# A preLN graph layer on one core: last batch's sums on another queue, its backward product by halves, two first batches reordered

## What is computed

```python
A_fwd = [adj, adj, shifted]                  # shifted = roll(eye, 1, axis=0)
A_list = A_fwd + [swapaxes(a, 1, 2) for a in A_fwd] + [eye]
HW = einsum('bnf,rfo->rbno', h, W[:, :F]) + einsum('rd,rdo->ro', W_edges, W[:, F:])[:, None, None, :]
out = x + max(einsum('rbnm,rbmo->rbno', A, HW), axis=0) + b
```

## Time and profile before

| | us |
|---|---|
| three runs | 214.88, 215.05, 215.61 |
| median | 215.05 |
| the profiled execution | 214.69 |
| its span, from first to last instruction | 212.9 |
| busy: PE, DVE, ACT, POOL | 203.8, 195.0, 182.8, 168.2 |
| TensorE's granted clock | 1.0 throughout |

### The profile page before, as it was taken

One profiled execution on the slowest core, in us unless ns is written; L12 is line 12 of the kernel. 1 busy time (PEld: TensorE's weight loads), 2 busy tenths in 40 slices (PEclk: granted clock), 3 DMA queues, 4 the chain that ended last, 5 costly groups with the idle time before them and its releaser, 6 DMA issues.

```text
span 212.9 us, 5004 instructions
## 1 busy us (share of the span) xinstructions
PE 203.8 (96%) x1003; PEld 165.4 (78%) x1003; DVE 195.0 (92%) x416; ACT 182.8 (86%) x453; POOL 168.2 (79%) x181
## 2 busy tenths in 40 slices
PE   7899998999999999999999999999999999999972
PEld 5677786877888888888888888888888888888851
DVE  4799779999999999999999999999999999989754
ACT  4779999699898989899998989999898989998360
POOL 1356869959797997979798897979799797979340
PEclk9999999999999999999999999999999999999999
DMA  6999879896998889797989989897988988053614
GB/s 226 299 334 198 123 153 293 187 278 97 338 158 250 190 241 248 180 269 124 292 161 236 211 213 272 170 261 132 261 184 215 251 191 229 3 143 57 145 53 99
DMA packets 117776, 42.38 MB, mean 199 GB/s; under 512 B 97287, under 2 KB 107527, under 8 KB 117767
## 3 DMA queue, kind: packets, MB, share of 16 engines
q1 hardware_dynamic: 113728, 33.11, 68.6%
q10 hardware_dynamic: 4039, 9.17, 13.6%
HBM read 38.00 MB, written 4.26 MB: 199 GB/s over the span
## 4 chain that ended last, share of the span: by engine, by line
PE 78%; DVE 6%; issue 4%; ACT 4%; DMA 4%; ACTq 1%; POOL 1%; DVEq 0%; POOLq 0%
PE rel_ps L880 11%; PE rel_ps L882 10%; PE rel_ps L881 10%; PE at_ps L857 9%; PE fwd_ps L880 6%; PE fwd_ps L882 6%; PE fwd_ps L881 6%; PE bwd_ps L882 6%; PE bwd_ps L880 6%; PE bwd_ps L881 5%; PE turn_ps L865 3%; DVE best L699 2%; DMA sum_all<-sums_dram 2%; DMA x_sb<-in_x 1%; ACT rel_ps L505 1%
## 5 line engine op out<-in xcount | busy, mean ns | idle before, releaser
L341 POOL TENSOR_TENSOR a_lo<-a_sb,a_hi 128x512 fp32r<-128x512 f32 x61 | 78.2, 1304 | 21.7 <-ACT a_hi L429 21.7
L505 ACT ACTIVATE rel_ps<-sum_all,c_col 128x512 f32<-128x512 f32 (+1 forms) x63 | 41.9, 685 | 10.5 <-DVE best L699 6.2
L699 DVE TENSOR_TENSOR best<-rel_ps,best 128x512 f32<-128x512 f32 x62 | 42.3, 682 | 2.3 <-PE rel_ps L882 1.7
L429 ACT ACTIVATE a_hi<-a_sb 128x512 fp32r<-128x512 f32 x64 | 39.5, 633 | 2.0 <-DMA a_sb<-in_adj 2.0
L670 DVE TENSOR_TENSOR at_lo<-at_ps,at_hi 128x512 fp32r<-128x512 f32 x48 | 32.7, 684 | 2.8 <-ACT at_hi L442 2.5
L442 ACT ACTIVATE at_hi<-at_ps 128x512 fp32r<-128x512 f32 x48 | 28.3, 591 | 5.7 <-PE at_ps L857 5.1
L880 PE MATMUL fwd_ps<-at_hi,h_hi 128*128 128x512 f32 x64 | 26.7, 417 | 0.7 <-issue 0.5
L880 PE MATMUL bwd_ps<-a_hi,h_hi 128*128 128x512 f32 x64 | 26.5, 414 | 0.0
L857 PEld LDWEIGHTS at_ps<-ident,a_sb 128*128 128x128 f32 x184 | 22.0, 141 | 4.6 <-issue 0.4
L857 PE MATMUL at_ps<-ident,a_sb 128*128 128x128 f32 x184 | 25.3, 272 | 0.0
L882 PE MATMUL fwd_ps<-at_hi,h_lo 128*128 128x512 f32 x64 | 25.3, 395 | 0.0
(11 more groups left out here) (107 smaller groups left out, 473.1 us busy)
## 6 DMA issues: line engine op xcount, KB each, us to landing
a_sb<-in_adj SPq DMA_DIRECT2D x28, 512.0 KB, 4.3
sum_all<-sums_dram ACTq DMA_DIRECT2D x16, 512.0 KB, 5.0
x_sb<-in_x SPq DMA_DIRECT2D x16, 256.0 KB, 5.2
xp_sb<-in_x SPq DMA_DIRECT2D x60, 64.0 KB, 3.2
out<-o_sb SPq DMA_DIRECT2D x60, 64.0 KB, 4.4
a_blocks<-in_adj SPq DMA_DIRECT2D x56, 64.0 KB, 2.1
a_sb<-in_adj SPq DMA_DIRECT2D x6, 256.0 KB, 4.5
sums_dram<-sum_rows ACTq DMA_DIRECT2D x56, 1.0 KB
```

What stands on the lines that cost most here:

```text
L341: pool.tensor_tensor(a_lo[q][:, j, :], a_sb[q][:, j, :], a_hi[q][:, j, :].bitcast(fp32), ALU.subtract).then_inc(a_lo_ready[j], 1)
L429: act.activation(a_hi[q][:, j, :], a_sb[q][:, j, :], ACT.Copy, accum_out=sums[q][:, j:j + 1]).then_inc(a_hi_ready[j], 1)
L505: act.activation(to[:, cols], sum_all[q][:, 0 if r in FWD else 1, cols], ACT.Copy, scale=c_col[:, r:r + 1]).then_inc(after_it, 1)
L699: dve.tensor_tensor(best[q][:], held[:], best[q][:], ALU.max).then_inc(joined[r], 1)
```

## The change

Five things are changed.

1. In the last step VectorE turns the sums ahead of the split of the last turned block (`turn_sums` between `split_at` 2 and 3), and SP, not ScalarE, stores and spreads the sums of batch 15. SP does this ahead of storing the output of batch 13; the load of the bias by nodes also comes ahead of that.
2. The `bwd` product of batch 15 is made in two halves of the nodes, half 0 in `bwd_ps` and half 1 in `turn_ps`, chunk by chunk between the relations of batch 14. Rounding, split and the relations 3 and 4 follow by halves, each in a bank of its own (`half_bank`).
3. The joins of batch 15 are ordered: relation 0, halves 0 of relations 3 and 4, relation 1 whole, halves 1 of relations 3 and 4. TensorE and ScalarE follow that order.
4. In batches 0 and 1: ScalarE rounds the first turned block ahead of the last chunk of a, spreads the sums of batch 0 behind the next block, and stores those of batch 1 behind all of normalise; VectorE does bn_stats of batch 3 ahead of taking the sums, and bn_aggr behind `split_ht`.
5. SP waits for the store of batch 0's sums ahead of `load_a_blocks(1, 0)`.

```diff
-        half_filled, half_done, half_stored = sem("half_filled"), sem("half_done"), sem("half_stored")
+        half_stored = sem("half_stored")
...
+        bwd_half_done, bwd_half_hi_ready, bwd_half_lo_ready = (
+            pair(sem, s) for s in ("bwd_half_done", "bwd_half_hi_ready", "bwd_half_lo_ready"))
+        half_done = {r: pair(sem, f"half_done{r}_") for r in BWD}
+        half_filled = {r: pair(sem, f"half_filled{r}_") for r in BWD}
+        part_joined = sem("part_joined")
+        bwd_half = (bwd_ps, turn_ps)
+
+        half_bank = {BWD[0]: (fwd_ps, rel_ps[BANK[FWD[0]]]), BWD[1]: (rel_ps[BANK[EYE[2]]], fwd_ps)}
...
+
+        def store_sums(queue, k, q):
+
+            queue.wait_ge(sum_rows_ready, 2 * k + q + 1)
+            for g in range(G):
+                queue.dma_start(sums_dram[q][:, g * Q:(g + 1) * Q],
+                                sum_rows[q][g * Q:g * Q + S, :]).then_inc(sums_stored[q], 16)
+
+        def spread_sums(queue, k, q):
+
+            queue.wait_ge(sums_stored[q], 16 + G * 16 * k)
+
+            wait(queue, filled[BWD[1]], 2 * k + q - 1)
+            queue.dma_start(sum_all[q][:].rearrange("p t n -> p (t n)"),
+                            sums_dram[q].rearrange("s p -> (s p)").unsqueeze(0).to_broadcast([P, 2 * N])
+                            ).then_inc(sums_spread[q], 16)
...
                 reload_x(0, 0)
                 reload_a(0, 0)
+
+                sp.wait_ge(sums_stored[0], 16)
                 load_a_blocks(1, 0)
...
             step(PAIRS - 1, 0, False)
-            step(PAIRS - 1, 1, False)
 
             sp.wait_ge(a_lo_ready[0], B - 1)
             sp.wait_ge(a_turned[C - 2], B - 1)
             sp.dma_start(last_bias.rearrange("p (c o) -> p c o", o=O), by_nodes(bias)).then_inc(bias_by_nodes_loaded, 16)
+
+            store_sums(sp, PAIRS - 1, 1)
+            spread_sums(sp, PAIRS - 1, 1)
+            step(PAIRS - 1, 1, False)
             store(PAIRS - 1, 0)
             store_half(sp, 0)
...
                 for j in range(C):
-                    if is_batch(b, 2) and j == C // 2:
-                        store_first_sums(1)
                     last = act.activation(h_sb[q][:, j, :], x_sb[q][:, j, :], ACT.Relu,
                                           bias=shift[q][:, j:j + 1], scale=rstd[q][:, j:j + 1])
                 last.then_inc(h_ready, 1)
...
-                spread_sums(0, 0)
                 round_at(*ahead, 2)
+                spread_sums(act, 0, 0)
                 round_ht(*ahead)
                 round_at(*ahead, 3)
                 round_a(*ahead, 0)
...
                     normalise(*ahead)
-                if not second:
-                    store_sums(k, q)
+                if second:
+                    store_first_sums(1)
+                elif left:
+                    store_sums(act, k, q)
                 act.wait_ge(joined[FWD[0]], b)
                 fill(*prev, BWD[0], rel_ps[BANK[BWD[0]]], filled[BWD[0]])
...
             round_a(0, 0, 2)
+            round_at(0, 0, 0)
             round_a(0, 0, 3)
-            for i in range(C):
+            for i in range(1, C):
                 round_at(0, 0, i)
             round_ht(0, 0)
...
+            def round_bwd_half(half):
+                act.wait_ge(bwd_half_done[half], 1)
+                act.activation(bwd_hi[:, half_cols(half)], bwd_half[half][:, half_cols(half)],
+                               ACT.Copy).then_inc(bwd_half_hi_ready[half], 1)
+
             act.wait_ge(joined[BWD[0]], B - 1)
             fill(k, q, FWD[0], rel_ps[BANK[FWD[0]]], filled[FWD[0]])
+            act.wait_ge(fwd_lo_ready, B)
+            fill(k, q, BWD[0], half_bank[BWD[0]][0], half_filled[BWD[0]][0], half_cols(0))
+            act.wait_ge(rel_done[BWD[1]], B - 1)
+            round_bwd_half(0)
             act.wait_ge(joined[BWD[1]], B - 1)
             fill(k, q, FWD[1], rel_ps[BANK[FWD[1]]], filled[FWD[1]])
-            act.wait_ge(fwd_lo_ready, B)
-            fill(k, q, BWD[0], fwd_ps, filled[BWD[0]])
-            round_bwd(k, q)
             act.wait_ge(joined[EYE[2]], B)
-            fill(k, q, BWD[1], rel_ps[BANK[EYE[2]]], half_filled, slice(0, HALF))
-            act.wait_ge(bwd_lo_ready, B)
-            fill(k, q, BWD[1], bwd_ps, filled[BWD[1]], slice(HALF, N))
+            fill(k, q, BWD[1], half_bank[BWD[1]][0], half_filled[BWD[1]][0], half_cols(0))
+            round_bwd_half(1)
+            act.wait_ge(joined[FWD[0]], B)
+            fill(k, q, BWD[0], half_bank[BWD[0]][1], half_filled[BWD[0]][1], half_cols(1))
+            act.wait_ge(part_joined, 1)
+            fill(k, q, BWD[1], half_bank[BWD[1]][1], half_filled[BWD[1]][1], half_cols(1))
             store_half(act, 1)
...
+            def split_bwd_half(half):
+
+                dve.wait_ge(bwd_half_hi_ready[half], 1)
+                dve.tensor_tensor(bwd_lo[:, half_cols(half)], bwd_half[half][:, half_cols(half)],
+                                  bwd_hi[:, half_cols(half)].bitcast(fp32), ALU.subtract).then_inc(bwd_half_lo_ready[half], 1)
...
                     split_at(k, q, 2)
+                    if not left:
+                        turn_sums(k, q)
                     split_at(k, q, 3)
-                    turn_sums(k, q)
+                    if left:
+                        turn_sums(k, q)
...
                 join(*prev, FWD[0])
                 if is_batch(b, 1):
+                    moments(k + 1, q)
                     take_sums()
                     join(*prev, FWD[1])
...
                     split_fwd(k, q)
-                if left > 1:
+                if left > 1 and not is_batch(b, 1):
                     moments(k + 1, q)
                 join(*prev, BWD[0])
                 if left > 1:
                     dve.wait_ge(bn_done, b + 3)
                 if left:
                     split_at(*ahead, 1)
-                if left > 1:
+                if left > 1 and not is_batch(b, 1):
                     mean_and_variance(q)
                 if left:
                     split_fwd(k, q)
+                if not left:
+                    split_bwd_half(0)
                 join(*prev, BWD[1])
                 if left:
                     split_ht(*ahead)
                 else:
                     turn_best(*prev)
+                if is_batch(b, 1):
+                    mean_and_variance(q)
                 join(k, q, EYE[2])
                 if left:
                     turn_best(*prev)
...
-            split_bwd(k, q)
+            split_bwd_half(1)
             join(k, q, FWD[0])
-            join(k, q, FWD[1])
-            join(k, q, BWD[0], fwd_ps)
-            dve.wait_ge(joined[BWD[0]], B)
-            for half, (held, done, count) in enumerate(((rel_ps[BANK[EYE[2]]], half_done, 1),
-                                                        (bwd_ps, rel_done[BWD[1]], B))):
...
+            dve.wait_ge(joined[FWD[0]], B)
+
+            def join_half(r, half, joined_ahead, joined_now):
+                cols = half_cols(half)
+                dve.wait_ge(half_done[r][half], 1)
+                dve.wait_ge(*joined_ahead)
+                dve.tensor_tensor(best[q][:, cols], half_bank[r][half][:, cols], best[q][:, cols],
+                                  ALU.max).then_inc(joined_now, 1)
+
+            join_half(BWD[0], 0, (joined[FWD[0]], B), part_joined)
+            join_half(BWD[1], 0, (part_joined, 1), part_joined)
+            dve.wait_ge(part_joined, 2)
+            dve.wait_ge(rel_done[FWD[1]], B)
+            dve.tensor_tensor(best[q][:], rel_ps[BANK[FWD[1]]][:], best[q][:], ALU.max).then_inc(half_joined[0], 1)
+            join_half(BWD[0], 1, (half_joined[0], 1), part_joined)
+            join_half(BWD[1], 1, (part_joined, 3), half_joined[1])
...
+            def bwd_half_chunk(half, j):
+
+                q = 1
+                if half == 0:
+                    if j == 0:
+                        pe.wait_ge(h_hi_ready, B)
+                        pe.wait_ge(h_lo_ready, B)
+                        pe.wait_ge(bwd_lo_ready, B - 1)
+                    pe.wait_ge(a_hi_ready[j], B)
+                    pe.wait_ge(a_lo_ready[j], B)
+                elif j == 0:
+                    pe.wait_ge(ht_lo_ready, B)
+                cols = half_cols(half)
+                last = passes(bwd_half[half][:, cols], h_hi[q][:, j, :], h_lo[q][:, j, :],
+                              a_hi[q][:, j, cols], a_lo[q][:, j, cols], j == 0, j == C - 1)
+                if j == C - 1:
+                    last.then_inc(bwd_half_done[half], 1)
...
+                elif not left:
+                    bwd_half_chunk(0, 0)
+                    bwd_half_chunk(0, 1)
+                    along(*prev, BWD[0])
+                    bwd_half_chunk(0, 2)
+                    bwd_half_chunk(0, 3)
+                    along(*prev, BWD[1])
+                    bwd_half_chunk(1, 0)
+                    bwd_half_chunk(1, 1)
+                    eye(k, q, EYE[2])
+                    bwd_half_chunk(1, 2)
+                    bwd_half_chunk(1, 3)
```

(24 more changed lines are left out.)

19 lines of the change are left out of this document (3 added, 16 removed).

## The result

| | before | after |
|---|---|---|
| median of six runs | 215.09 us (214.43 to 215.61) | 212.94 us (212.62 to 213.59) |
| ratio, with 95% interval | | 0.9904 (0.9878 to 0.9930) |
| profiled execution, and its span | 214.69, 212.9 | 212.62, 210.8 |
| busy: PE, DVE, ACT, POOL | 203.8, 195.0, 182.8, 168.2 | 203.9, 193.1, 183.8, 168.9 |

The direction was right and the size wrong: 212.94 lies 0.56 us under the range. The end cost what its sum said. The start gained 2.16 us where 1.0 was forecast.

What follows compares the result with a forecast made beforehand. TensorE, busy for 96% of the span, was taken as the bound, so gains must come from the first batches or the end: 214.69 - 1.0 + 0.25 = 213.94 us profiled, 214.3 against the median, range 213.5 to 215.6.

Steps and rivals of the forecast that it cites:

- The end, +0.25 forecast: Last batch: first fill 2.3 us sooner, but 8.65 us instead of 6.13 from it to the last join: 0.25 us net cost.
- the prediction's own list of signs of being wrong: Signs: TensorE waits for a_sb or h_lo, first fill waits for the spread, gaps in the middle, no idle VectorE before half split.
- The rival of a gain at the end: Last batch: half instructions overlap better, the end gives 0.3 and the start its full 1.15, total 213.6 us; chance 15%.
- the late landing: Last batch: sums land at 201.4 and the end costs 0.8, total 214.9 us; one case of the cancelling rival, 25%.
- The start, 1.0 forecast: First batches: 1.15 us gained by ScalarE's and VectorE's order, 0.15 taken off for the adjacency of batch 3.
- spread of batch 0 behind at_hi 2, and the gate: First batches: moving the spread frees ScalarE of 0.5, but its landing (18.2 and the median 5.0) stays the bound: no gain.
- ScalarE's and VectorE's order, "1.15 us": Batches 1 and 2: uninterrupted normalise and moved bn_stats and bn_aggr bring VectorE's results sooner; TensorE gains 1.15 us.
- adjacency of batch 3, "I take 0.15 off": SP's later loads bring the adjacency at 38.5 instead of 36.3, just when TensorE wants it; 0.15 us taken off.
- The product of 34.65: TensorE, batch 2: this product, which waited for VectorE, was to start at about 33.5, a gain of 1.15 us.
- The first rival (216.0): SP's gate frees nothing: loads come 3.8 us later, batch 3's adjacency at 40.1, start loses 0.5 to 0.9; chance 15%.
- The rule on the order of completions: Skill's rule: a semaphore's increment lands only after all earlier writes of that DMA engine across queues; then the gate frees 1.6 us.
- the turn at 32.33: TensorE's turn in batch 2, 0.60 us long, taken as floor: the work behind it starts at 32.8 instead of 33.41.

Runs made afterwards that it cites:

- bn_pool: Changed kernel with the statistics steps (bn_stats, bn_aggr) back in their old places on VectorE and GpSimd's wait in all batches: 213.38 us, ratio 0.9919.
- after_pool: Changed kernel plus GpSimd's wait for VectorE's difference of the turned quarter in all batches: 212.70 us, ratio 0.9885.
- pool_waits: Kernel before plus one wait: in batches 2 to 15 GpSimd starts its differences only after VectorE's of the turned quarter: 213.81 us, ratio 0.9916.
- cast_first: Kernel before, but in batch 1 GpSimd does its sum of input and bias behind the difference of the features: 215.02 us, ratio 0.9988.
- no_gate: Changed kernel without SP's wait for the store of the first sums: 213.62 us, ratio 0.9933.

## Why the prediction was right or wrong

**The end, +0.25 forecast, +0.27 measured (17.13 against 16.86).** Right in size at each step: rows ready sooner, issue by SP, landing near 3.8 (3.96), first fill 2.3 sooner (198.89 from a mark at 190.32 is 8.57, before 10.73: 2.16), 8.65 us of queue behind it (8.56), VectorE idle 1.5 and 0.8 (1.68 and 0.85). One thing is otherwise, and it is on the prediction's own list of signs of being wrong: the first fill does wait for the spread, 0.95 us. The forecast had batch 14's relation 3 as the later of the two; its join ended at 198.63, the spread landed at 198.81. That is where the 0.14 went that the fill lacks of its 2.3. The means of all profiles, 16.96 against 16.72, bear out the cost. The rival of a gain at the end fell with it, as did the late landing.

**The start, 1.0 forecast, 2.16 measured.** The failed step is this sum. It put the first mark at nothing, it had no term at all for the length of VectorE's instructions beside GpSimd's, and its other two terms were 0.14 and 0.15 short:

| step of the prediction | forecast | measured | what the runs showed |
|---|---|---|---|
| spread of batch 0 behind at_hi 2, and the gate: "its landing stays the bound there: nothing" | 0 | 0.39 | first fill at 22.71 instead of 23.08, spread issued at 17.41 instead of 18.23; ten profiles with the new order have a median turn of 32.0, seven with the old one 32.65 |
| ScalarE's and VectorE's order, "1.15 us" | 1.15 | 1.29 | "1 to 2"; bn_stats and bn_aggr are 0.65 of it (bn_pool against after_pool) |
| not in the sum: VectorE's SBUF instructions beside GpSimd | 0 | 0.48 | "2 to 3" and "3 to 4"; pool_waits gives 0.50 there |
| adjacency of batch 3, "I take 0.15 off" | -0.15 | 0 | issued 3.6 later (forecast 2.2), but under way for 5.3 us, not 7.3: there at 37.85, 0.1 ahead of the transposes |
| sum | 1.00 | 2.16 | |

The first term fails by the prediction's own numbers. It had the store of the first sums land at 16.6 instead of 18.2, and still let the spread, which waits for that store, start from 18.2. In the kernel before ScalarE stood 0.50 us for that store and 0.18 for the spread; in the changed kernel it stands for neither, but for 0.06 us ahead of the fill.

The second was right. The product of 34.65 was forecast 1.15 sooner, and came at 33.08, 1.18 sooner behind its turn. The rest of the 1.29 is the restart: after a wait TensorE's next product begins 0.33 behind (34.65 to 34.98), without one 0.23.

The third is the one that could have been read. The row of 1.74 us stood in the trace beside 48 of 0.65 to 0.69 with PSUM as input and twelve of its own kind of 0.68 to 0.70, and I took the 1.79 of the last batch as the instruction's own length. One shortcut of 1.07 us in VectorE's queue became 0.5 on TensorE.

The Trainium skill, "SBUF — State Buffer", section "Who interferes with whom", says that a VectorE instruction with two inputs in SBUF contends with one of GpSimd that reads SBUF, and that a cast can be in a mode that contends with GpSimd too, where whoever issues first has the shared ports for its whole instruction and the other blocks. By that rule the cast of 27.88 would wait for GpSimd's row of 27.59, to 28.89, and then take its 0.43: an estimate of 1.44 from its start. The trace has 1.30, so it agrees to 0.14 us. pool_waits and cast_first are what shows it here.

The fourth was near the edge. The adjacency was there 0.1 us ahead of its use in this execution, the fastest of six, and in five of the nine profiles with the gate it was late by 0.13 to 0.76. That nothing was lost here is luck; the limit that the prediction feared is real.

**The gate.** Forecast: the store of the first sums lands at 16.6 instead of 18.2. With the gate SP's next load shows the landing, since it waits for it: 15.92 in the changed kernel, 15.8 to 17.5 in the nine profiles with it. So the store was indeed sooner there. But the start doesn't gain all of that: ScalarE's queue reaches the spread at 17.4 only, and without the gate (no_gate) the store had landed by then as well. So it isn't shown that the gate is what made the store sooner. The first rival (216.0) named the right place, the adjacency of batch 3, but had it under way for as long as before; issued 3.6 later it landed 2.0 sooner after its issue. The rule on the order of completions that the prediction weighed is neither borne out nor refuted by these runs.

**Chances.** 43% for faster was too little for a start whose second term was right; the likeliest cases all put the start at 1.15 at most, because the turn at 32.33 was taken as a floor that the change can't move. It moved by 0.39.

**What remains open.** What the gate is worth, what SP's queue is worth without the early turn, why a later adjacency lands quicker, and how much of the first mark is the change: the spread was issued between 17.54 and 18.50 in the seven profiles with the old order, between 17.41 and 18.36 in the ten with the new one, so the 0.39 of one pair of profiles may be partly chance.

## What to carry to other kernels

Where one operation on one shape has two lengths in a trace, look at what GpSimd (or VectorE) had begun just before: the longer one is a lost race, and a wait on the engine that has time to spare can win it for the other. A gain in such a length counts only where somebody waits for it, so try it at the place where the chain passes. Before the difference of two stretches is given to an edit, look for a wait at their end that belongs to something else: here the adjacency, up to 0.76 us. A split made finer for overlap is worth nothing if its first piece stands in an ordered queue ahead of work that is ready; move the piece behind that work first, and then see whether the finer split still pays.

## What the hardware showed that I had not expected

- A 128x512 difference of VectorE from two SBUF tiles took 0.66 to 0.69 us alone and 1.60 to 1.80 where GpSimd's had begun first; the cast of the same size 0.43 against 1.27 to 1.54, and 0.68 to 0.82 where GpSimd's was further on. GpSimd's pair of differences went from 2.53 to 3.00 at the same time: both lose.
- Transfers that are issued later can land sooner: 512 KB of adjacency issued at 28.76 was under way for up to 9.0 us, issued at 32.05 for up to 5.3.
- The spread of the sums took 3.96 and 4.45 us at the end, but from 18.02 it was under way until ScalarE's fill at 24.05 in pool_waits. The first batches follow it: the turn lies between 31.70 and 33.30 in the 17 profiles.
